# A graph network's attention stage: rounding moved ahead of a normalisation, two VectorE items reordered, a wait moved

## What is computed

```python
h = relu(layernorm(x))
q, k, v = h @ Wq + bq, h @ Wk + bk, h @ Wv + bv
adj = zeros((N, N)).at[src, dst].set(1.0)
a = q @ k.T / sqrt(512)
x = x + softmax(a * adj + (1 - adj) * -1e6) @ v
h = relu(layernorm(x))
agg = segment_sum(h[src], dst); deg = max(segment_sum(1, dst), 1)
x = x + alpha * (agg / deg[:, None] @ W.T + b)
```

## Time and profile before

| what | value |
|---|---|
| median of three runs | 235.61 us |
| the profiled execution, its own time | 236.24 us |
| its span in the trace | 234.5 us |
| mean granted TensorE clock | 0.993 |
| TensorE matmuls, busy share | 96% |
| VectorE | 74% |
| ScalarE | 40% |
| GpSimd | 33% |

### The profile page before, as it was taken

One profiled execution on the slowest core, in us unless ns is written; L12 is line 12 of the kernel. 1 busy time (PEld: TensorE's weight loads), 2 busy tenths in 40 slices (PEclk: granted clock), 3 DMA queues, 4 the chain that ended last, 5 costly groups with the idle time before them and its releaser, 6 DMA issues.

```text
span 234.5 us, 3313 instructions
## 1 busy us (share of the span) xinstructions
PE 226.2 (96%) x1226; PEld 182.9 (78%) x1226; DVE 173.3 (74%) x282; ACT 94.2 (40%) x175; POOL 76.3 (33%) x106
## 2 busy tenths in 40 slices
PE   8999999999999999998999999999689999999995
PEld 6576788988878888886888888887558888888884
DVE  5988999999989755779999998886753662073222
ACT  3669928634213150445564644545035002060000
POOL 4266035620000049961045736324345106000000
PEclk9999999999999999999999999999799999999999
DMA  6999101000000020011212111111004000001232
GB/s 181 361 392 402 58 3 46 0 0 3 0 3 0 0 74 21 24 46 51 54 51 53 46 51 34 40 31 46 22 4 175 0 0 3 3 0 45 111 115 90
DMA packets 11762, 15.47 MB, mean 66 GB/s; under 512 B 2656, under 2 KB 6752, under 8 KB 11616
## 3 DMA queue, kind: packets, MB, share of 16 engines
q1 hardware_dynamic: 10880, 14.83, 19.2%
q10 hardware_dynamic: 864, 0.40, 0.6%
HBM read 9.97 MB, written 2.10 MB: 51 GB/s over the span
## 4 chain that ended last, share of the span: by engine, by line
PE 84%; DVE 8%; issue 3%; ACT 3%; POOL 1%; ACTq 0%; DVEq 0%; POOLq 0%
PE bank L858 19%; PE bank L1015 13%; PE bank L847 12%; PE bank L849 12%; PE bank L848 12%; PE bank L874 8%; PE bank L931 3%; PE bank L924 3%; DVE dsum L803 2%; DVE negmax L772 2%; PE bank L908 1%; DVE pT_lo L776 1%; DVE pr L769 1%; PE bank L842 1%; ACT pr L527 1%
## 5 line engine op out<-in xcount | busy, mean ns | idle before, releaser
L847 PE MATMUL bank<-V_hi,pT_hi 128*128 128x512 f32 x64 | 25.7, 401 | 3.4 <-DVE pT_lo L776 3.4
L1015 PE MATMUL bank<-A,h_hi 128*128 128x512 f32 x64 | 25.0, 391 | 1.1 <-DVE pT_lo L776 1.1
L848 PE MATMUL bank<-V_lo,pT_hi 128*128 128x512 f32 x64 | 25.6, 400 | 0.0
L849 PE MATMUL bank<-V_hi,pT_lo 128*128 128x512 f32 x64 | 25.6, 400 | 0.0
L596 DVE TENSOR_TENSOR ohL<-iotaL,lo_b 128x1024 bf16<-128x1024 bf16 x33 | 22.6, 684 | 3.8 <-PE bank L874 3.7
L600 DVE TENSOR_TENSOR ohW<-iotaW,key_b 128x1280 bf16<-128x1280 bf16 (+4 forms) x33 | 25.1, 760 | 0.0
L847 PE MATMUL bank<-hT_hi,GT_hi 128*128 128x512 f32 x64 | 25.0, 391 | 0.0
L849 PE MATMUL bank<-hT_hi,GT_lo 128*128 128x512 f32 x64 | 24.9, 389 | 0.0
L1015 PE MATMUL bank<-A,h_lo 128*128 128x512 f32 x64 | 24.9, 389 | 0.0
L848 PE MATMUL bank<-hT_lo,GT_hi 128*128 128x512 f32 x64 | 24.9, 389 | 0.0
L874 PEld LDWEIGHTS bank<-ohW,ohL 128*128 128x128 bf16 x334 | 18.6, 98 | 3.9 <-issue 3.3
(11 more groups left out here) (133 smaller groups left out, 502.4 us busy)
## 6 DMA issues: line engine op xcount, KB each, us to landing
pT_f<-turned SPq DMA_DIRECT2D x96, 32.0 KB, 1.9
xs<-in_x SPq DMA_DIRECT2D x4, 512.0 KB, 7.6
out_dram<-o_sb SPq DMA_DIRECT2D x7, 256.0 KB, 2.0
wv_raw<-in_wv SPq DMA_DIRECT2D x1, 1024.0 KB, 11.1
wk_rows<-in_wk SPq DMA_DIRECT2D x1, 1024.0 KB, 13.0
wq_rows<-in_wq SPq DMA_DIRECT2D x1, 1024.0 KB, 12.1
wt_raw<-in_wT SPq DMA_DIRECT2D x1, 1024.0 KB, 5.3
wq_raw<-in_wqT SPq DMA_DIRECT2D x3, 256.0 KB, 7.4
```

The source lines that it names most:

```text
L847: mm(out, lhs[0][a], rhs[0][b], start=(first and k == 0), stop=False)
L848: mm(out, lhs[0][a], rhs[1][b], start=False, stop=False)
L849: last = mm(out, lhs[1][a], rhs[0][b], start=False, stop=(final and k == len(pairs) - 1))
L1015: last = mm(bank[AGG_BANK[n]][:, :], h2[hl][:, h, m * P:(m + 1) * P], A[:, h, half * HALF:(half + 1) * HALF], start=(h == 0 and hl == 0), ...
```

## The change

On ScalarE high(j) moves: it was the first step of round j+2, and is now the step behind the copies of row j+1, ahead of the normalisation of row j-2. Only high(7) stays behind the normalisation of row 5. On VectorE low(0) moves from behind to ahead of the maximum of row 2 (the other low parts keep their place), and the degree sums of block 7 move from the end of round 7 to the end of round 8. On TensorE the wait for the last low part moves from ahead of the aggregate to behind the degree matmuls. No instruction is added or removed.

```diff
--- before.py
+++ after.py
@@ -514,14 +514,15 @@
                         act.wait_ge(dots, n + 1)
                         nc.scalar.activation(V[0][:, n, :], ps[:, :], ACT.Copy).then_inc(proj_hi, 1)
 
+            def high(j):
+
+                act.wait_ge(own_blocks, NQ * (j + 1))
+                act.wait_ge(pT_in[j % 2], 16 * NQ * (NQ - 1) * (j // 2 + 1))
+                if j >= 2:
+                    act.wait_ge(attended, j - 1)
+                nc.scalar.activation(by_quarter(pT[j % 2][0]), pT_f[j % 2][:, :, :, :], ACT.Copy).then_inc(pT_hi, 1)
+
             for i in range(NT + 3):
-                if 2 <= i < NT + 2:
-                    j = i - 2
-                    act.wait_ge(own_blocks, NQ * (j + 1))
-                    act.wait_ge(pT_in[j % 2], 16 * NQ * (NQ - 1) * (j // 2 + 1))
-                    if j >= 2:
-                        act.wait_ge(attended, j - 1)
-                    nc.scalar.activation(by_quarter(pT[j % 2][0]), pT_f[j % 2][:, :, :, :], ACT.Copy).then_inc(pT_hi, 1)
                 if i < NT:
                     act.wait_ge(maxed, i + 1)
                     nc.scalar.activation(pr[i % 2][:, :], pr[i % 2][:, :], ACT.Exp, bias=negmax[:, i:i + 1],
@@ -534,6 +535,8 @@
                         rows = slice(a * Q, (a + 1) * Q)
                         nc.scalar.activation(pT_f[i % 2][rows, a, :, :], turned[i % 2][rows, a, :, :],
                                              ACT.Copy).then_inc(own_blocks, 1)
+                if 1 <= i < NT:
+                    high(i - 1)
                 if i == NT + 2:
                     act.wait_ge(ld_wt, 16)
                     nc.scalar.activation(wt[0][:, :, :], wt_raw[:, :, :], ACT.Copy).then_inc(w_hi, 1)
@@ -545,6 +548,8 @@
                     norm_relu(1, j, h2f[j % 2][:, :])
                     act.wait_ge(relu, NT + j + 1)
                     nc.scalar.activation(h2[0][:, j, :], h2f[j % 2][:, :], ACT.Copy).then_inc(h2_hi, 1)
+                if i == NT:
+                    high(NT - 1)
 
             for n in range(2 * KD):
                 half, m = n // KD, n % KD
@@ -759,6 +764,19 @@
                 dve.wait_ge(h2_hi, j + 1)
                 nc.vector.tensor_tensor(h2[1][:, j, :], h2f[j % 2][:, :], f(h2[0][:, j, :]), ALU.subtract).then_inc(h2_lo, 1)
 
+            def degree_sums(i):
+
+                with nc.allow_low_precision(reason="whole numbers below EXACT where every edge is in its window"):
+                    nc.vector.tensor_reduce(dsum[:, i * P:(i + 1) * P],
+                                            A_f[:, :, i * P:(i + 1) * P].rearrange("p h d -> p d h"),
+                                            AX.X, ALU.add).then_inc(deg_sums, 1)
+
+            def low(j):
+
+                dve.wait_ge(pT_hi, j + 1)
+                nc.vector.tensor_tensor(by_quarter(pT[j % 2][1]), pT_f[j % 2][:, :, :, :], f(by_quarter(pT[j % 2][0])),
+                                        ALU.subtract).then_inc(pT_lo, 1)
+
             for i in range(NT + 3):
                 if i < NT:
 
@@ -768,13 +786,12 @@
                         cols = slice(q * HALF, (q + 1) * HALF)
                         ins = nc.vector.copy_predicated(pr[i % 2][:, cols], A_i[:, i, cols], bank[score_bank(i, q)][:, :])
                         ins.then_inc(masked, 1)
+                    if i == 2:
+                        low(0)
                     dve.wait_ge(masked, 2 * i + 2)
                     nc.vector.tensor_reduce(negmax[:, i:i + 1], pr[i % 2][:, :], AX.X, ALU.max, negate=True).then_inc(maxed, 1)
-                if 2 <= i < NT + 2:
-                    j = i - 2
-                    dve.wait_ge(pT_hi, j + 1)
-                    nc.vector.tensor_tensor(by_quarter(pT[j % 2][1]), pT_f[j % 2][:, :, :, :], f(by_quarter(pT[j % 2][0])),
-                                            ALU.subtract).then_inc(pT_lo, 1)
+                if 3 <= i < NT + 2:
+                    low(i - 2)
                 if i < NT:
                     if i >= 2:
                         dve.wait_ge(pT_in[i % 2], 16 * NQ * (NQ - 1) * (i // 2))
@@ -798,11 +815,10 @@
                                                    in1=xs[:, j, :], op0=ALU.mult, op1=ALU.add).then_inc(x2_ready, 1)
                     dve.wait_ge(x2_ready, j + 1)
                     row_stats(j)
-                if i < NT:
-                    with nc.allow_low_precision(reason="whole numbers below EXACT where every edge is in its window"):
-                        nc.vector.tensor_reduce(dsum[:, i * P:(i + 1) * P],
-                                                A_f[:, :, i * P:(i + 1) * P].rearrange("p h d -> p d h"),
-                                                AX.X, ALU.add).then_inc(deg_sums, 1)
+                if i < NT - 1:
+                    degree_sums(i)
+                if i == NT:
+                    degree_sums(NT - 1)
             h2_lo_part(NT - 1)
 
 
@@ -1023,7 +1039,8 @@
                     scores(i)
                 if i >= 3:
                     j = i - 3
-                    pe.wait_ge(pT_lo, j + 1)
+                    if j < NT - 1:
+                        pe.wait_ge(pT_lo, j + 1)
                     if j == 0:
                         pe.wait_ge(counts_final, 1)
                     if j >= 2:
@@ -1034,6 +1051,7 @@
                         pe.wait_ge(deg_sums, NT)
                         degrees([dsum[:, 0:HALF]], 0, True, True)
                         degrees([dsum[:, HALF:N]], 1, True, True).then_inc(deg_ps, 1)
+                        pe.wait_ge(pT_lo, NT)
                     three_pass(bank[6 + j % 2][:, :], pT[j % 2], V,
                                [((every, b, every), (every, b, every)) for b in range(NT)]).then_inc(attended, 1)
```

## The result

| | before | after |
|---|---|---|
| median | 236.06 us (4 runs) | 229.40 us (4 runs, 228.90 to 230.24) |
| the profiled execution, its own time | 236.24 us | 230.24 us |
| its span | 234.5 us | 228.5 us |
| mean TensorE clock | 0.993 | 1.000 |

The ratio is 0.9712, with a 95% interval of 0.9657 to 0.9768: 6.8 us faster, 5.5 to 8.1. Forecast were 229.1 us and a gain of 6.6.

What follows compares the result with a forecast made beforehand. TensorE was taken as the bound, with time to win only where it stands or runs slower. 0.78 + 2.65 + 3.20 = 6.63 us off the 235.61 median gives 228.98, plus 0.1 for small waits: 229.1 us, range 228.2 to 230.8.

Steps and rivals of the forecast that it cites:

- The three losses: TensorE's lost time in the attention stage: 1.08 us at attention 0, 2.65 at attention 6, 3.06 before the aggregate.
- First edit: VectorE's low(0) ahead of the maximum of row 2: TensorE's first wait shrinks from 1.08 to 0.30, -0.78 us.
- Its price: VectorE's later work for rows 2 and 3 comes 1.50 us later; cost taken 0, bound above 0.5 us.
- Second edit: ScalarE's high(j) ahead of the normalisation of row j-2: attention 6's wait and the slow stretch go, -2.65 us.
- Third edit: VectorE's degree sums of row 7 one round later, so that low(6) can start about 160.3; cost 0.
- Fourth edit: TensorE awaits the last low part behind the degree matmuls: aggregate at 168.11 instead of 174.60, -3.20 us in this part.
- The slow clock: TensorE's clock of 0.50 from 168.0 to 170.5 follows the 2.65 us standstill and goes with it.
- Rival 1: Tail late because low(6) delays GpSimd's operations by 1.2 us: 229.5, or 230.3 if low(7) is 2 us late; chance 0.12.
- Rivals 2 and 3: Attention 6's wait stays in part, 230.1 or 231 to 232, chance 0.08; VectorE's lag grows, about 237, chance 0.02.

Runs made afterwards that it cites:

- split queue: Changed kernel with three of row 0's twelve transfers issued from ScalarE's queue instead of SyncE's: 229.06 us, ratio 0.9711.
- edit 1 alone: Kernel before with only VectorE's low(0) moved ahead of the maximum of row 2: 235.03 us, ratio 0.9934.
- Without edit 4: Kernel before with only ScalarE's rounding ahead of the older normalisation and the last degree sums one round later: 236.11 us, ratio 0.9974.
- edit 4 alone: Kernel before with only TensorE's wait for the last low part moved behind the degree matmuls: 234.58 us, ratio 0.9899.
- the added wait: Changed kernel with one wait more, attention 6 also awaiting x2 of row 5: 232.18 us, ratio 0.9838.
- without edit 2: Changed kernel with ScalarE's rounding of row j back behind the normalisation of row j-2: 234.03 us, ratio 0.9898.
- the changed kernel without edit 4: Changed kernel with TensorE's wait for the last low part back ahead of the aggregate: 235.25 us, ratio 0.9951.

## Why the prediction was right, point by point

- **The three losses**. Right: they were the only thing to win, and two are gone wholly, the third in part. Nothing between them became shorter.
- **First edit, -0.78 us: mis-sized.** It measured -0.46 and -0.30 in the two traces of the changed kernel and -0.56 alone. The step that failed is "so it doesn't move" for high(0). It hangs on the last of twelve transfers, and that landed for a start of high(0) at 106.25 instead of 105.75, 0.32 us later when counted from scores 0, which is the whole of 0.78 - 0.46. I took its start from one execution as fixed, though the row itself says that a transfer released it. In the kernel before, the maximum of row 2 stood between and covered that; the edit made the transfer the last to come. The table bears it out: in the three kernels without edit 1 attention 0 begins at 22.97 to 22.99, in the nine traces with it and one queue at 22.18 to 22.67. The earliest, 0.79 us ahead of before, is the one in which high(0) started at 19.81 as it did before (104.72 - 84.91); so the forecast 0.78 is what the edit gives when that queue is no slower. The split queue shows it too: with the transfers early, attention 0 gains 22.97 - 21.89 = 1.08 us against before, the whole loss.
- **Its price: a lag without cost, right; the lag itself was larger.** low(1) went from 114.72 to 116.72, 1.8 us later counted from scores 0 where 1.50 was forecast (low(0) too began 0.3 us later than in the sum), and nothing waited; edit 1 alone carries its gain to the last matmul (0.52 us).
- **Second edit, -2.65 us, and the clock: right** in the company of edit 4, -2.65 -3.20 forecast against 6.27 - 0.46 = 5.81 measured. The second trace gives 6.12 - 0.30 = 5.82. Without edit 4 it is worth little or nothing (236.11 against 236.34). I had written the sum as terms that could each be read alone; the text on the fourth edit did hold the reason (low(7) at 170.5 to 171.5 while attention 6 ends at 168.1), but didn't say that a kernel with edit 2 only would stand there.
- **Third edit, cost 0: right, its reason wrong.** I said that it lets low(6) start in time. Without it low(6) is in time too, by 0.5 us.
- **Fourth edit: right.** low(7) ended at 172.89, TensorE wanted it at 180, and the aggregate's own inputs were in time. Forecast was an end at 170.5 to 171.5: high(7) started at 169.64 instead of 168.2, as the chain ahead of it had lost 1.1 us at rstd (below). The cover of 8 us took that in.
- **The slow clock follows the standstill: only partly shown.** After the change there is none and the clock is at 1.000 in all ten executions; in all 47 of the kernel before beside the experiments it was 0.991 to 0.993. It was 0.992 or 0.993 also in all nine executions with edit 1 alone or edit 4 alone, which list 2.50 and 2.49 us. But with the added wait, which is half a microsecond shorter, it fell in one of five, and without edit 2, where the wait is as long as before, in three of four (0.991 to 0.993; the fourth 1.000, and 232.61 us). So it follows a standstill of this length nearly always, not always. What decides is open; each execution's mean clock is known, but the length of its standstill only for the profiled one.
- **Rival 1, the late tail: its mechanism came, its price didn't.** rstd took 1.65 us instead of 0.57, the chain behind was later, and x2 of row 7 ended at 187.16, 1.2 us later than in the sum. The sum had left it 0.74 us of cover; TensorE too came 0.56 us later than in the sum (at 187.25, not 186.69), of which 0.32 is the first edit and 0.18 the earlier part of this execution. So 0.09 us of cover was left. The sum put this meeting at nothing, and that it cost no wait is a matter of a tenth of a microsecond and not of the reason given (that small operations fit in between): the margin held, narrowly. The weight load did wait, hidden behind matmuls (waits from 165 to 190 us):

```profile
PEld bank L1031 <- DVE xs L814: 0.2, 1, 0.2
```

  The rule of the Trainium skill (SBUF — State Buffer, "Who interferes with whom") that the prediction set against the change holds here for GpSimd: a VectorE instruction with two inputs in SBUF and a GpSimd instruction that reads SBUF contend, and the order in which they start decides. The rows are rstd's 1.65 beside a low(6) of 1.23, against 0.57 with a degree sum, which has one input, in its place; and where rstd started first, by 0.01 us in the changed kernel without edit 4, it took 0.57 and the next operation, nmr, was held:

```profile
159.78 0.57 POOL L388 TENSOR_TENSOR rstd<-var_e,nhalf 128x1 f32<-128x1 f32 x1
160.45 0.73 POOL L402 TENSOR_SCALAR nmr<-mv,rstd 128x1 f32<-128x1 f32 x1
...
159.79 1.25 DVE L777 TENSOR_TENSOR pT_lo<-pT_f,pT_hi 128x1024 fp32r<-128x1024 f32 x1 [0.41 <-ACT pT_hi L523]
```

  But the rule in the prediction's form, that the two block each other wholly whoever is first, holds one way only in this meeting: low(6) took 1.23 to 1.25 us in the four traces where rstd of 0.57 us started first, so VectorE wasn't held. By a longer GpSimd operation it was: low(7) from 170.72 on took 2.17 us beside an addition of 1.29 us that had begun at 170.53. Why the short one didn't hold it is open.
- **Rivals 2 and 3** didn't occur: no wait at attention 6, no mask late.
- **The total**: 229.1 forecast, 229.40 measured. The first edit fell 0.3 us short in the trace; the medians themselves spread by more than that (229.40 and 229.95 for the same kernel), so their nearness is in part luck.

## What to carry to other kernels

When an engine that is the bound waits twice in a row for the same kind of input, removing the first wait alone moves the time to the second; look at what the second really needs (here the aggregate read nothing of what it waited for) and move both. A wait's releaser in the profile names who came last, not who comes next to last: before an instruction is moved up to the moment its input is there, follow that input back to its own releaser, here a queue that issues one transfer each 0.63 us, with one long issue that differs from execution to execution. And an edit's worth should be told with the others present and absent; here the fourth was worth 1.5 us alone and over 5 with the rest.

## What the runs showed of the hardware

- A GpSimd operation on 128x1 elements took 0.57 us alone and 1.65 when VectorE's subtraction of 1.23 us, with two inputs in SBUF, started in the same 0.01 us. Where the GpSimd operation was the first by 0.01 to 0.07 us (four traces), it took 0.57, the next one 0.73 to 0.75 instead of 0.27, and the subtraction its usual 1.23 to 1.25.
- TensorE's clock fell in all 47 executions of the kernel before, whose standstill is listed with 2.49 us in its trace; in all nine with edit 1 alone (2.50) or edit 4 alone (2.49); in three of four with the same 2.49 us and edits 1, 3 and 4; in one of five with 1.99 us; in none of four with 1.13 us. Behind a fall the 24 matmuls of attention 6 took 7.14 to 7.19 us instead of 5.44, and 5.57 behind the 1.13 us without one.
- SyncE's queue issues twelve transfers of 32 KB one by one, each 0.63 us behind the last, except that one of the twelve issues took longer: 1.09 us in the trace of the kernel before, 1.40 and 1.56 in the two of the changed kernel.
- With 4.04 us of standstill the clock fell in ten of ten executions, and in two of them the lower level lasted longer (mean clock 0.985 and 0.986, against 0.992 or 0.993): about 6 us in the profiled one, where 50 matmuls took 14.33 us instead of 11.34. With 3.47 us it fell in ten of ten too, longer in three (0.985), and the 50 matmuls took 13.99 us.
